# Two groups of products with the values in a row, with ten exponential buffers, in a two-layer gated cross-attention kernel

## The reference

```python
Q = (queries @ W_q.T).reshape(b, sq, N_HEADS, D_HEAD).transpose(0, 2, 1, 3)
K = (keys @ W_k.T)...   ;  V = (values @ W_v.T)...
scores = jnp.einsum('bhqd,bhkd->bhqk', Q, K) / scale
scores = jnp.where(mask, scores, NEG_INF)          # layer 0 only
attention = jax.nn.softmax(scores, axis=-1)
heads_out = jnp.einsum('bhqk,bhkd->bhqd', attention, V)
x = x + jnp.tanh(g) * (heads_out @ W_proj.T + b_proj)
```

## Time and profile before

| what | value |
|---|---|
| median of 3 runs | 1285.3 us |
| lowest, highest | 1281.34, 1289.36 us |
| span of the profiled execution | 1284.1 us |
| TensorE busy | 1213.3 us, 94% of the span |
| VectorE, ScalarE busy | 893.2 and 710.7 us |
| TensorE's mean granted clock | 0.987 |

### The profile page before, as it was taken

The page is one execution under the profiler, slowest core; times in us unless marked ns, Lnnn a source line. Parts: engine busy times, 40 slices in busy tenths (PEclk is TensorE's granted clock), DMA queues, the critical chain, the costliest instruction groups (busy, mean ns, idle before and its releaser), DMA issues.

```text
span 1284.1 us, 25175 instructions
## 1 busy us (share of the span) xinstructions
PE 1213.3 (94%) x9260; PEld 859.1 (67%) x9260; DVE 893.2 (70%) x2680; ACT 710.7 (55%) x1197; POOL 481.3 (37%) x675
## 2 busy tenths in 40 slices
PE   7899999999999989999999989999999999988998
PEld 6577666666767654444458866677676776578987
DVE  4677677876787646589999856767867868652333
ACT  2455555555655538889973426666566566622221
POOL 5534333443443100067000334344643643322555
PEclk9899999999999999999999999999999999998999
DMA  6423333233432041000004653355455342137973
GB/s 194 127 77 105 91 93 108 88 105 98 123 88 67 11 128 55 1 1 2 1 1 130 177 157 108 108 152 147 129 167 136 113 134 72 51 145 241 311 194 39
DMA packets 121942, 137.22 MB, mean 107 GB/s; under 512 B 12882, under 2 KB 116428, under 8 KB 121798
## 3 DMA queue, kind: packets, MB, share of 16 engines
q1 hardware_dynamic: 111888, 125.98, 33.2%
q0 software_dynamic: 7296, 8.15, 3.5%
q10 hardware_dynamic: 2634, 1.49, 0.5%
HBM read 58.42 MB, written 27.36 MB: 67 GB/s over the span
## 4 chain that ended last, share of the span: by engine, by line
PE 55%; DVE 6%; issue 3%; ACT 2%; POOL 1%; SPq 1%; DMA 1%; ACTq 0%; POOLq 0%; DVEq 0%
PE PS L669 14%; PE PS L715 6%; PE PS L470 5%; PE PS L410 5%; PE PS L683 4%; PE PS L453 4%; PE PS L429 4%; PE PS L528 2%; PE PS L724 2%; PE PS L502 2%; PE PS L417 2%; DVE NM L1119 1%; PE PS L546 1%; ACT P L839 1%; PE PS L511 1%
## 5 line engine op out<-in xcount | busy, mean ns | idle before, releaser
L839 ACT ACTIVATE P<-PS 128x512 f32<-128x512 f32 x512 | 302.4, 601 | 165.8 <-PE PS L456 100.2
L1116 DVE CUSTOM_DVE_ANT_0 MX<-PS,NQ 128x256 bf16<-128x256 f32 x512 | 192.5, 418 | 73.3 <-PE PS L429 73.0
L453 PE MATMUL PS<-QS,KS 99*128 99x256 bf16 x1024 | 226.6, 275 | 7.7 <-ACT P L839 6.7
L1119 DVE TENSOR_REDUCE NM<-PS 128x2 f32<-128x512 f32 x256 | 173.5, 685 | 74.6 <-PE PS L429 72.9
L429 PE MATMUL PS<-KS,QS 96*128 96x256 bf16 x1024 | 196.9, 275 | 21.6 <-DVE NM L1116 13.4
L429 PEld LDWEIGHTS PS<-KS,QS 96*128 96x128 bf16 x1024 | 87.2, 98 | 86.6 <-DVE NM L1116 26.1
L470 PE MATMUL PS<-P,V 128*32 128x256 f32 x2048 | 137.7, 387 | 1.5 <-ACT P L839 1.5
L453 PEld LDWEIGHTS PS<-QS,KS 99*128 99x128 bf16 x1024 | 95.4, 99 | 53.3 <-ACT P L839 20.1
L456 PE MATMUL PS<-NK,identb 128*128 128x256 bf16 x512 | 128.2, 275 | 0.0
L669 PE MATMUL PS<-XNT,wup 128*128 128x512 f16 x576 | 124.9, 379 | 0.0
L669 PEld LDWEIGHTS PS<-XNT,wup 128*128 128x128 f16 x576 | 56.2, 98 | 67.3
(11 more groups left out here) (233 smaller groups left out, 2473.6 us busy)
## 6 DMA issues: line engine op xcount, KB each, us to landing
KS<-PP SPq DMA_DIRECT2D x192, 128.0 KB, 2.9
QS<-PP SPq DMA_DIRECT2D x192, 128.0 KB, 2.5
WH<-in_wex SPq DMA_DIRECT2D x16, 768.0 KB, 8.0
WG<-in_wex SPq DMA_DIRECT2D x10, 768.0 KB, 5.1
bufd<-bias_row SPq DMA_DIRECT2D x5, 1032.0 KB, 12.0
XB<-in_x SPq DMA_DIRECT2D x16, 256.0 KB, 2.8
CT<-in_ctxT SPq DMA_DIRECT2D x16, 256.0 KB, 3.1
x1d<-XB SPq DMA_DIRECT2D x16, 256.0 KB, 2.1
```

Source lines behind the costliest of these rows:

```text
L453: ins = tensor.matmul(o, t.KS[b % 3][0:99, h, 128 * kt:128 * kt + 128], t.QS[b % 3][0:99, h, :], start=True, stop=(L == 1))
L839: scalar.activation(t.P[h % 8][:, :, :], PS[:, h % 2, :].rearrange("p (k n) -> p k n", k=2), ACT.Exp).then_inc(s_ex, 1)
L1116: ins = vector.tensor_tensor_reduce(t.MX[:, 2 * (h % 2) + qt, :], PS[:, bk, 256 * qt:256 * qt + 256], t.NQ[b % 4][:, qt, :], -1.0, 1.0e30, ...
L1119: ins = vector.tensor_reduce(nm[:, :, h], PS[:, bk, :].rearrange("p (t n) -> p t n", t=2), X, ALU.max, negate=True)
```

## The change

Groups 0 and 1 are now multiplied one after the other in slot 9, and groups 2 and 3 in slot 1 of the next step, instead of one each in slots 5, 9, 13 and 1. P has ten buffers instead of eight, taken in turn over all heads of all batches, and an exponential waits for the group that last read its buffer. OT has one buffer instead of two, and its writer waits for both transposes of the batch before. The memory is the same: two P of 2 KB a partition for one OT of 4 KB.

```diff
@@ -27,6 +27,7 @@
 QMAX = 32767.0
 NCH = 24
 UR = 8
+NP = 10
 PARTS = ((0, 0), (0, 1), (1, 0))
 GROUPS = [(0, 4), (4, 4), (8, 4), (12, 2), (14, 1), (15, 1)]
 
@@ -224,8 +225,8 @@
 
             t.QS, t.KS = ([None] + [stack(f"{w}S{i}") for i in (1, 2)] for w in "QK")
             t.V = [tile(m, f"V{i}", [128, 2, H, 32], F32) for i in range(3)]
-            t.P = [tile(m, f"P{i}", [128, 2, 256], F32) for i in range(8)]
-            t.OT = [tile(m, f"OT{i}", [128, 4, 256], F32) for i in range(2)]
+            t.P = [tile(m, f"P{i}", [128, 2, 256], F32) for i in range(NP)]
+            t.OT = tile(m, "OT", [128, 4, 256], F32)
             t.ON = tile(m, "ON", [128, 2, 256], F32)
             t.ONT = tile(m, "ONT", [128, 2, 256], F32)
             t.RD = tile(m, "RD", [128, 2, H], F32)
@@ -468,7 +469,7 @@
                 for i in range(4):
                     h = 4 * g + i
                     ins = tensor.matmul(PS[32 * i:32 * i + 32, ob, 256 * (g % 2):256 * (g % 2) + 256],
-                                        t.V[b % 3][:, kt, h, :], t.P[h % 8][:, kt, :], start=(kt == 0), stop=(kt == 1))
+                                        t.V[b % 3][:, kt, h, :], t.P[(16 * n + h) % NP][:, kt, :], start=(kt == 0), stop=(kt == 1))
             ins.then_inc(s_ah, 1)
 
         def pe_keys(L, b):
@@ -508,7 +509,7 @@
             bk = odd_bank(("on", n, qt), s_on, 2 * n + qt + 1)
             pe.wait_ge(s_ot, 2 * n + 2)
             for g in range(4):
-                ins = tensor.transpose(PS[:, bk, 128 * g:128 * g + 128], t.OT[b % 2][:, g, 128 * qt:128 * qt + 128],
+                ins = tensor.transpose(PS[:, bk, 128 * g:128 * g + 128], t.OT[:, g, 128 * qt:128 * qt + 128],
                                        ident[:, :])
             ins.then_inc(s_otr, 1)
 
@@ -561,8 +562,9 @@
         def pe_slot(L, s, k):
             if 0 <= s < NB:
                 pe_scores_t(L, s, k)
-                if k in (5, 9, 13):
-                    pe_av(L, s, (k - 5) // 4)
+                if k == 9:
+                    pe_av(L, s, 0)
+                    pe_av(L, s, 1)
             if 0 <= s + 1 < NB:
                 if (L, s, k) == (1, -1, 2):
                     pe_warm(5, 8)
@@ -585,6 +587,7 @@
                     pe_values(L, b)
             if 0 <= s - 1 < NB:
                 if k == 1:
+                    pe_av(L, s - 1, 2)
                     pe_av(L, s - 1, 3)
                 if k in (5, 6):
                     pe_heads(L, s - 1, k - 5)
@@ -834,16 +837,17 @@
         def act_exp(L, b, h):
             n, t = L * NB + b, TL[L]
             i = 16 * n + h
-            act.wait_ge(s_ah, 4 * n + h // 4 - 1)
+            if i >= NP:
+                act.wait_ge(s_ah, (i - NP) // 4 + 1)
             act.wait_ge(s_st, i + 1)
-            scalar.activation(t.P[h % 8][:, :, :], PS[:, h % 2, :].rearrange("p (k n) -> p k n", k=2),
+            scalar.activation(t.P[i % NP][:, :, :], PS[:, h % 2, :].rearrange("p (k n) -> p k n", k=2),
                               ACT.Exp).then_inc(s_ex, 1)
 
         def act_heads(L, b, hh):
             n, t = L * NB + b, TL[L]
-            act.wait_ge(s_otr, 2 * (n - 1))
+            act.wait_ge(s_otr, 2 * n)
             act.wait_ge(s_ah, 4 * n + 2 * hh + 2)
-            scalar.activation(t.OT[b % 2][:, 2 * hh:2 * hh + 2, :], PS[:, 4 + hh, :].rearrange("p (g n) -> p g n", g=2),
+            scalar.activation(t.OT[:, 2 * hh:2 * hh + 2, :], PS[:, 4 + hh, :].rearrange("p (g n) -> p g n", g=2),
                               ACT.Copy).then_inc(s_ot, 1)
 
         def act_maxima(L, b, hh):
```

## The result

The changed kernel takes 1297.3 us (median of 4 runs, 1294.2 to 1299.2), the kernel before 1285.0 beside it (4 runs). The ratio is 1.009, with a 95% interval of 1.0064 to 1.0116: slower, by 8 to 15 us. What follows is about the 8.9; where the other 3.4 us lie no trace shows.

A forecast was written before the change was run, and what follows sets the result against it. It took TensorE's in-order queue (94% busy) as the bound, VectorE and ScalarE right behind. Layer 1 +8.3 and +0.9, layer 0 +3.1, ends +0.5 gave +12.8 on 1285.3: 1298 us, range 1280 to 1312.

The forecast's parts named there:

- A pair: TensorE, slots 9 and 1: a group alone costs 1.10 us, a second behind it 0.87, so 0.23 saved.
- Rival 2: A pair saves nothing, the second group entering as dearly as the first: 1313 us, chance 0.12.
- Slot 5: Layer 1: removing group 0 gives back 0.59 of 1.10 us; TensorE waits 0.51 for OT.
- The hand-over: From ScalarE to TensorE, taken as about 0.05 us; 0.15 would add 0.2 a batch in layer 1.
- Slot 13: Layer 1: removing group 2 gives back 0.40 of 1.10 us; TensorE waits 0.70 for head 11's maximum.
- The batch of layer 1: Slots 1, 5, 9 and 13 summed to +0.75 us on 23.1; eleven such batches gave +8.3.
- The batches with routing work: Layer 1: three batches where VectorE is already late in slots 10 to 13, +0.3 us each, +0.9 together.
- Layer 0: Fourteen batches at +0.39 us up to slot 10, less 2.4 in all behind it: +3.1 us.
- the wait of slot 0: Layer 0: waits away TensorE's gain since slot 10's residual in half the batches; seven others keep 2.4 us in all.
- Ends: First batches save a group's move without loss, last ones get a pair with nothing to hide it: together +0.5 us.
- Rival 1: The pairs' saving shows and the new waits don't, the moved groups being no cover: 1271 us, chance 0.13.
- Rival 3: New waits replace present ones in layer 1, or layer 0 gains what layer 1 loses: +3, 1288 us, chance 0.19.

The follow-up runs named there:

- e4: Changed kernel with ScalarE's second copy into OT moved from slot 3 to the end of slot 2: 1298.6 us beside 1288.2 before, ratio 1.008.
- e5: Changed kernel with VectorE's residual moved from the end of slot 10 to slot 11, behind its maximum: 1307.7 us beside 1285.2 before.
- e10: Changed kernel with early OT copy, division ahead of rounding in slot 5, and value projection ahead of slot 13's score product: 1289.0 us beside 1287.5 before.
- e11: e10 with VectorE's normalisations of slots 13 and 14 each a slot later: 1273.7 us beside 1287.5 for the kernel before, ratio 0.9894.
- e2: Changed kernel with only groups 0 and 1 paired; group 2 back in slot 13, group 3 in slot 1: 1283.7 us beside 1288.2 before.
- e3: Changed kernel with only groups 2 and 3 paired; group 0 back in slot 5, group 1 in slot 9: 1305.7 us beside 1288.2 before.

## Why the prediction was right

**The time.** Forecast 1298, measured 1297.3; by spans the change is +8.9 us where the sum had +12.8. That the medians meet to 0.7 us is in part luck: the sum was made from a trace, and against the trace it is 3.9 us too high, while the medians lie 3.4 us further apart than the two profiled executions. Sign, size and both waits were right.

**A pair.** Forecast 1.00 + 0.87, measured 1.87 in the trace. Rival 2 is out by that row; TensorE's busy time fell by 8.8 us, less than the 14.7 of the sum, but a row's busy time runs past the start of the next and isn't the measure of that saving. Entry and exit are paid once for a pair. This fits the drain that the Trainium skill (TensorEngine Tiling (Array Packing), Key Properties) ties to a change of tiling mode; the trace shows the cost, 0.23 us, and not the drain itself.

**Slot 5.** Forecast -0.59 and a wait of 0.51 us for OT; measured -0.67 over slots 5 to 7, and L512 0.60 late. The hand-over took 0.15 us and not 0.05, so slot 5 itself gave only 0.48 (1.98 to 1.50); slot 7 gave another 0.23 (1.50 to 1.27), since the router's product no longer waits for ON, and slot 6 lost 0.04. So the size was right by two errors against each other, and the reason was half: OT stood in front of a second limit, ON behind the rounding, that I hadn't looked for. By e4 the three slots take the same time when OT comes early.

**Slot 13.** Forecast -0.40 and a wait of 0.70; measured -0.39 and 0.70. The sentence that slots 14 to 0 have room enough held for the change itself (slot 0 stayed at 2.16), but not by much: e5 and e10 took 0.6 to 0.7 us out of slot 13 and got it back in slot 0. The group was covering a stretch of VectorE's queue (5.2 us in e10), not one maximum.

**The batch of layer 1.** Forecast +0.75, measured +0.66; layer 1 as a whole +9.2 forecast without its ends, +8.5 measured with them. The batches with routing work were forecast at +0.3; two of them went from 25.18 to 25.39 and 25.38. Of the others most grew by 0.66, the second by 1.10 and two by 0.90.

**Layer 0.** Forecast +3.1, measured +0.3 for the whole stretch, and -0.2 a batch in the mean of twelve where the sum had +0.22 (0.39 - 0.17). The mis-sized term is the wait of slot 0: I let TensorE lose there all that it gained in slot 13 less VectorE's idle time, 0.79 - 0.17 = 0.62 us; the means show slot 0 longer by 0.25. The others came as priced: slot 13 -0.83 (forecast -0.79), slot 10 -0.35 (-0.28), the second groups +0.87 and +0.79 (+0.87 each), slots 5 to 7 -0.93 (-1.07).

**Ends.** Forecast +0.5. The last full interval of layer 0 grew from 21.7 to 23.1 and that of layer 1 from 19.4 to 20.2 us, the first ones shrank by 0.7 and 0.45: +1.1.

**The rivals.** Rival 1 (1271 us, the saving without the waits) is near what e11 comes to at 1273.7 beside 1287.5, after four kinds of work were moved (the copy, the division, the values, the normalisations); the change as made doesn't have it. Rival 3 is out in both of its forms: the new waits came on top of the present ones, and layer 0 didn't gain what layer 1 lost (+0.3 beside +8.5), though in e2 it does (-4.6 beside +2.8).

## What to carry to other kernels

Work that an in-order engine does between issuing a tile and needing the answer is cover. Before moving it, measure at the place it leaves how late each answer comes, not only the first: the second limit stands hidden behind the first, and freeing one alone shows nothing. A pair of groups that saves 0.23 us was worth having where the answers came in time, and a loss where they didn't; splitting the change by place (e2, e3) showed this at once. Where waits follow each other closely, look at the granted clock behind them before putting the whole loss down to waiting. When a removed wait comes back some slots later with the same size, the thing to shorten is the other engine's queue between the two places.

## What was not expected

The two halves of the change, -0.36% and +1.37%, differ by over 20 us while their sum, +1.0%, is close to the change's +0.9%. In the steady batch of layer 1 they add up exactly, +0.19 and +0.47 us for +0.66; over the whole layer they don't, +2.8 and +13.8 for +8.5, in part since e3 lost the full clock in places where the change didn't. And VectorE, about 70% busy over the span, bounds slots 10 to 0 of a layer 1 batch once TensorE waits no more in slot 13: moving two normalisations of 0.4 us each behind the next maximum took 0.64 us from a steady batch and 15 us from the kernel (e11 against e10).
